# A message stage on one core: TensorE's first two layers one group further ahead, two ScalarE copies moved, sums stored an iteration later

## The reference, cut to what matters

```python
x = silu(edge_radial @ W1 + b1)          # layer 1: 8 -> 64
x = silu(x @ W2 + b2)                    # layer 2: 64 -> 64
tpw = x @ W3 + b3                        # layer 3: 64 -> 256
hs_e, hv_e = hs[src], hv[src]            # a gather: 32 features per edge
m0 = ALPHA * (einsum('eu,euw->ew', hs_e * sh0, W00) + INV_SQRT3 * einsum('eui,ei,euw->ew', hv_e, sh1, W110))
m1 = ALPHA * (einsum('eu,ei,euw->ewi', hs_e, sh1, W01) + einsum('eui,euw->ewi', hv_e * sh0, W10))
agg = segment_sum(concat(m0, m1), dst)   # then a residual and a layernorm
```

## Time and profile before

| | |
|---|---|
| median of 3 runs | 8405.06 us (8396.81 to 8455.76) |
| the profiled execution | 8418.97 us, its span 8417.1 us |
| busy over the span | PE 80%, DVE 76%, POOL 63%, ACT 33% |
| message stage | to about 4720 us |
| granted clock of TensorE, mean | 0.889 of full |

### The profile page before, as it was taken

One profiled execution on the slowest core, in us unless ns is written; L12 is line 12 of the kernel. 1 busy time (PEld: TensorE's weight loads), 2 busy tenths in 40 slices (PEclk: granted clock), 3 DMA queues, 4 the chain that ended last, 5 costly groups with the idle time before them and its releaser, 6 DMA issues.

```text
span 8417.1 us, 93644 instructions
## 1 busy us (share of the span) xinstructions
PE 6711.4 (80%) x26126; PEld 5190.8 (62%) x26126; DVE 6418.5 (76%) x11130; ACT 2817.8 (33%) x4982; POOL 5329.9 (63%) x5400
## 2 busy tenths in 40 slices
PE   6777777777777777777777409999999999999991
PEld 4555555555555555555555308888888888888881
DVE  7878887888888888887878437777777777777773
ACT  4455555555555555544444101111111111111110
POOL 5666666666666666665656566666666666666665
PEclk8888888888888888888888659999999999999995
DMA  2111111111111111111111102222222222222221
GB/s 62 41 38 42 42 42 41 41 41 40 42 42 42 42 42 41 41 38 33 35 34 35 45 24 45 48 48 50 51 48 48 51 51 48 48 49 52 48 48 27
DMA packets 318657, 363.23 MB, mean 43 GB/s; under 512 B 157446, under 2 KB 259510, under 8 KB 317962
## 3 DMA queue, kind: packets, MB, share of 16 engines
q0 software_dynamic: 175840, 136.07, 11.2%
q1 hardware_dynamic: 142794, 226.94, 8.5%
HBM read 251.38 MB, written 111.20 MB: 43 GB/s over the span
## 4 chain that ended last, share of the span: by engine, by line
PE 58%; issue 15%; another core or an unknown queue 11%; DVE 7%; ACT 6%; POOL 1%; DMA 0%; ACTq 0%; DVEq 0%; SPq 0%; POOLq 0%
PE tpw L664 29%; PE tpw L596 12%; PE hid L605 5%; PE hid L586 4%; PE hid L664 4%; PE hid L582 4%; ACT early L687 2%; ACT nearx L709 1%; ACT hid L681 1%; POOL starts L480 1%; DVE prod L964 1%; DVE hot L1255 1%; DVE early L976 1%; DVE msgs L1025 1%
## 5 line engine op out<-in xcount | busy, mean ns | idle before, releaser
L476 POOL DMA_INDIRECT early<-in_x_wide,idx x2870 | 2799.0, 975 | 1780.7 <-issue 1711.8
L476 POOL DMA_INDIRECT prod<-table,idx x2125 | 2140.7, 1007 | 1070.6 <-issue 590.2
L664 PE MATMUL tpw<-highs,hot 128*128 128x462 f32 x6125 | 2322.9, 379 | 81.1 <-DVE prod L1270 37.1
L664 PE MATMUL tpw<-lows,hot 128*128 128x462 f32 x6125 | 2302.4, 376 | 25.9 <-issue 25.2
L596 PE MATMUL tpw<-w3s,early 128*128 128x256 f32 x6252 | 1837.6, 454 | 9.4 <-DVE prod L964 9.0
L596 PEld LDWEIGHTS tpw<-w3s,early 128*128 128x128 f32 x6252 | 1379.9, 228 | 579.5 <-issue 339.0
L664 PEld LDWEIGHTS tpw<-highs,hot 128*128 128x128 f32 x6125 | 1173.0, 192 | 255.5 <-issue 58.3
L664 PEld LDWEIGHTS tpw<-lows,hot 128*128 128x128 f32 x6125 | 1167.3, 191 | 176.5 <-issue 46.4
L1270 DVE TENSOR_TENSOR prod<-tpw,mask 128x462 f32<-128x462 f32 x875 | 547.2, 637 | 540.4 <-remote 241.8
L687 ACT ACTIVATE early<-hid,b2s 64x384 f32<-64x384 f32 x1042 | 600.9, 577 | 932.8 <-PE hid L586 560.8
L582 PE MATMUL hid<-early,w1s 16*128 16x384 f32 x1044 | 552.7, 613 | 450.1 <-ACT early L687 368.8
(11 more groups left out here) (186 smaller groups left out, 7955.0 us busy)
## 6 DMA issues: line engine op xcount, KB each, us to landing
big<-qrows SPq DMA_DIRECT2D x126, 512.0 KB
scan<-prod SPq DMA_DIRECT2D x125, 425.0 KB
scan<-sums SPq DMA_DIRECT2D x130, 384.0 KB
early<-in_x_wide,idx POOLq DMA_INDIRECT x2870
prod<-table,idx POOLq DMA_INDIRECT x2125
qbx<-qx SPq DMA_DIRECT2D x131, 128.0 KB
early<-in_radial_t SPq DMA_DIRECT2D x262, 48.0 KB
sh<-in_sh SPq DMA_DIRECT2D x131, 48.0 KB
```

Source lines behind the costliest of these rows:

```text
L476: return pool.indirect_dma_start(out=dest, out_offset=None, in_=source, in_offset=bass.IndirectOffsetOnAxis(ap=index, axis=0))
L664: mm = pe.matmul(found[i % BANKS][:, 0:BC], hot(c)[:, g, at:at + P], split(s, g), start=g == 0 and s == 0, stop=g == NBATCH - 1 and s == S ...
```

## The change

PE runs layers 1 and 2 one group further ahead (`layer2(g + 2)`, `next_layer1(g + 3)`), ACT's two silus follow (`hidden(g + 2)`, `first_hidden(g + 3)`). ACT does `collect` and `spread_hv` of h1 in k1, and `spread_hv` of the next iteration's h0 in k3. POOL's wait on layer 1 names one group more. SP stores an iteration's sums after the refill two iterations later instead of one.

```diff
+            refill(1, 1, 1)
+            with sp.Fori(1, ITERS // 2 - 1) as pair:
                 for m in range(2):
-                    refill(pair * 2 + m + 1, 1 - m, 1 - m)
-                    store_sums(pair * 2 + m, m)
+                    refill(pair * 2 + m, m, m)
+                    store_sums(pair * 2 + m - 2, m)
...
                 if k % HALF == 0:
                     pool.wait_ge(tpw_ready, it * SLOTS + k - 1)
                 else:
-                    pool.wait_ge(layers_done, it * SLOTS + k)
+                    pool.wait_ge(layers_done, it * SLOTS + k + 1)
...
                     layer3(g, k % 2)
-                    layer2(g + 1)
+                    layer2(g + 2)
                     if finding and k % HALF == HALF - 1:
                         find_tile(it, m, k // HALF)
-                    next_layer1(g + 2, it + 1 if k + 2 >= SLOTS else it, (k + 2) % SLOTS)
+                    next_layer1(g + 3, it + 1 if k + 3 >= SLOTS else it, (k + 3) % SLOTS)
...
-                    hidden(g + 1, (k + 1) % 2)
-                    if k % HALF == 0:
-                        spread_hv(it, h, it > 1 if isinstance(it, int) else True)
-                    if k == 0 and before is not None:
-                        collect(it - 2, m, before, CT)
+                    hidden(g + 2, k % 2)
                     if k == 1:
+                        if before is not None:
+                            collect(it - 2, m, before, CT)
                         if first:
                             act.wait_ge(keep_ready, 1)
                         spread_keep(it, m, CT)
+                    if k % HALF == HALF - 1:
+                        spread_hv(it + 1 if h else it, 1 - h, h == 0 and before is not None or h == 1 and not first and not last,
+                                  last and h == 1)
                     if searching:
...
-                    first_hidden(g + 2)
+                    first_hidden(g + 3)
```

More of the change, by code:

```diff
@@ L406, in _ @@
                   .then_inc(qx_in[k], 16)
-            with sp.Fori(0, ITERS // 2 - 1) as pair:
+            refill(1, 1, 1)
+            with sp.Fori(1, ITERS // 2 - 1) as pair:
                 for m in range(2):
-                    refill(pair * 2 + m + 1, 1 - m, 1 - m)
-                    store_sums(pair * 2 + m, m)
+                    refill(pair * 2 + m, m, m)
+                    store_sums(pair * 2 + m - 2, m)
+            refill(ITERS - 2, 0, 0)
+            store_sums(ITERS - 4, 0)
             refill(ITERS - 1, 1)
+            store_sums(ITERS - 3, 1)
             sp.wait_ge(row_counted, SEARCHES)
@@ L622, in _ @@
             next_layer1(1, 0, 1)
+            layer2(1)
+            next_layer1(2, 0, 2)
             pe.wait_ge(w3_scaled, 1)
@@ L754, in collect, with iteration @@
                    .then_inc(sums_ready, 1)
-            def iteration(it, m, before, searching, loads=None):
+            def iteration(it, m, before, searching, loads=None, last=False):
                 first = before is None and m == 0
@@ L783, in _ @@
             first_hidden(1)
+            hidden(1, 1)
+            first_hidden(2)
+            spread_hv(0, 0, False)
             iteration(0, 0, None, True)
@@ L797, in _ @@
             iteration(ITERS - 2, 0, ITERS // 2 - 2, False, ITERS // 2 - 1)
-            iteration(ITERS - 1, 1, ITERS // 2 - 2, False)
-            spread_hv(ITERS, 0, False, True)
+            iteration(ITERS - 1, 1, ITERS // 2 - 2, False, None, True)
             collect(ITERS - 2, 0, ITERS // 2 - 1, CT)
```

## The result

| | us | iteration with the search | behind it | granted clock, whole run |
|---|---|---|---|---|
| before, median of 11 runs | 8405.7 | 35.9 | 36.0 | 0.889 |
| changed, median of 11 runs | 8482.4 | 36.8 | 35.9 | 0.856 |
| forecast | 8542 | 37.5 | 35.3 | |

The ratio is 1.0087, its 95% interval 1.0073 to 1.0102: slower by 77 us, which is real and just inside the 1% (84 us) that the prediction took as its bound. The profiled execution took 8500.6 us with a span of 8498.8, 81.7 more than before's span. The iterations account for it. With the starts of all of collect's rows it is 98 x (36.79 - 35.93) = +84 and 28 x (35.92 - 36.02) = -3, together +81.

What follows compares the result with a forecast made beforehand. A loop through VectorE, find_tile, layer 1, silus and spread_hv bounds it now; a loop between copies of h1 would follow. 98 x (37.5 - 35.9) = +157, 28 x (35.3 - 36.0) = -20: +137 on 8419, less 14: 8542 us, range 8200 to 8650.

Steps and rivals of the forecast that it cites:

- The new loop: From ScalarE's copy of h1 through silus, TensorE's layers and GpSimd's gathers to the next copy: 37.5 us with the search.
- The late signal: Layer 3 of k0' to GpSimd's first gather of h1: 5.64 us, part of it a signal late behind find_tile.
- the late signal goes: Rival at layer 3's signal to GpSimd: 2.4 us leave the loop; 8240 us, or some 7960 without clock cost; together 0.20.
- a first gather of h1 within 4 us of layer 3's start: On GpSimd behind layer 3 of k0': one of three signs that would show the prediction wrong; it took 5.64 us.
- The clock: TensorE runs at its lower level behind a 7 to 9 us pause, adding 2.5 us in layers 1 and 3.
- find_tile's stretch: On TensorE, from layer 2 of k1' through find_tile to layer 1 of k2': 0.91 + 2.98 us.
- The rival that combined them: Layer 3's signal no longer late, clock cost kept: iteration 35.1 and 32.9 us, 8240 us; 0.20 with the no-clock-cost case.
- Behind the search: Iterations after the node search: 34.05 us plus half the clock's cost, 1.25, gives 35.3; the pause a microsecond shorter.
- Collect: On ScalarE, moved to k1 before the copy of h1, where the engine would wait anyway: 2.11 us, costing nothing.
- SP's order: Stores moved back by one on SP's queue: nothing gained; unmoved, layer 1's input would come late.
- The gathers of h0: On GpSimd, landing 16 us behind the copy of h1: cost VectorE 1 to 2 us, but not the loop.
- "Remote" gone: Sign of being right, on ScalarE: the first silu no longer waits for TensorE's late layer 1 signal, 4.7 us before.

## Why the prediction was right, and where it was off

**The mechanism.** The new loop from one copy of h1 to the next sets the iteration: its terms add up in the trace (table above), it does not shorten without k1's gathers and does without k3's, and the copies taken out of it win 2.1%. The step "that closes a new loop" stands.

**The late signal, the step that was mis-sized first.** The prediction took 5.64 us from layer 3 of k0' to the first gather, "since the same instructions stand in the same order in front of it". It measured 3.62. The reason given was wrong: lateness does not come from find_tile ahead, but from the end of a run of gathers. In the kernel before layer 3's row ends at 2271.1, just as the last gather of h0' does (2271.21), and GpSimd goes on at 2273.88. In the changed kernel it ends at 2283.49 and the last gather at 2279.10. Nothing is left to hold it, and its semaphore rises at 2283.50. This is the rival "the late signal goes". It came true for this term and took 2.0 of its 2.4 us from the loop, and the prediction's own sign of being wrong, "a first gather of h1 within 4 us of layer 3's start", occurred.

**The clock, the step that was mis-sized second, the other way.** Forecast 2.5 us, measured 3.74, with the pause before it shorter (4.39 us here, 5.5 in the median) than the 7 to 9 forecast. The granted clock is 0.50 over 10.2 us, the lower level of 1.2 GHz throughout, not 0.55 over 6.6; it fell 1.1 us before the pause ended. So all but the last 0.5 us of layer 3 of k3 ran slowly, and layer 2, which the prediction's 2.5 left out. The section that the prediction named in the Trainium skill ("TensorE: Matmul & The Clock Gate", "HAM oscillation — how this bites in real kernels") has the burst behind the wait slow from its first matmul on, and here the trace agrees; its 2.8 with layer 2's 0.74 would have been 3.54.

The two errors, -2.0 and +1.2, with -0.3 on find_tile's stretch leave 36.4 for 37.5, and the forecast of +137 us became +77. That the forecast had the right sign is in part luck: with the signal's term alone put right the same sum has 35.5 and 33.3, 98 x -0.4 and 28 x -2.7, so some 115 us faster, and only the clock's error took that back. The rival that combined them (signal gone, clock paid) had 35.1; it missed by the clock's 1.2 us as well.

**Behind the search** 35.3 was forecast and 35.9 came. In 24 turns between 3800 and 4650 us the copy to the silu takes 2.33 us, 0.95 less as computed, and the gathers 12.86; layers 2 and 1 run as slowly as before, and the pause is 6.0 us in the median, not shorter. So halving the clock's cost was the error, 2 us or more, and the late signal that went hid most of it.

**Terms taken at nothing.** Collect: confirmed, since ScalarE still idles 3.31 and 5.94 us between spread_keep, which stands behind collect, and the copy of h1 in the turn above. SP's order: "if the queue were not moved, layer 1's input would come late" is true, at 890 us. The gathers of h0, "not the loop": true at 36.8, but they form a second loop at 34.1, which the prediction did not price. It bounded the kernel without k3's gathers and the one with layer 3 of k2 twice.

**The expected signs.** The copy of h1 waits for gathers in each of the 68 turns: yes, but 4.4 us in the median and not 5 or more (the 584.1 us hold the waits of h0's copy too). VectorE's waits at bsum, 300.7 us and another 182.6 in 47 waits that the profile puts down to issue, 6 us per iteration: yes. "Remote" gone: yes. Pauses of 7 us or more before one layer 2 per iteration: no, 5.5 in the median, and 7 or more in 10 of 68.

**What stays open.** Why a run of eleven gathers holds most of TensorE's signals near its end, which of them it lets pass, and by what means. The Trainium skill, "Perfetto Trace Analysis", section "Summary: the profiler window per engine type", says that a matmul's end in the profile is an estimate and that a software DMA's row ends with its descriptors, before the data has moved. By the first a late matmul would be possible too; the pairs of signals 0.13 us apart speak against it here. The second fits a release 2 us behind a gather's row, about when the copy finds the rows landed (2.41 us behind the last gather's start), and no run here separates the landing from the release. Nor were the moves of the two copies and of collect tried one at a time, and no run changed the clock alone.

## What to carry to other kernels

When a dependence is relaxed, write down the loop that closes next with every term from a row, and ask of each wait in it what else was going on at that moment: a late signal belonged here to another engine's gathers, not to the instruction ahead of it. A wait that looks idle may be pacing: letting GpSimd off its waits cost the changed kernel 5% and the one before 14%, and a store's place in a DMA queue cost 10%. Ask also which loop is second: the gain from the first ends there. TensorE's granted clock fell here from 0.87 to 0.77 when a quarter of its matmuls was cut, and the time stayed: price pauses and bursts, not matmuls.

## What the runs showed of the hardware

- In the kernel before, signals of TensorE that fall in the last 3 us of a run of gathers, or up to 1 us behind it, were late in 269 of 282 cases; the median release is 2.0 us behind the last gather's row. In the changed kernel it was 157 of 230. Where runs merge they were up to 12 us late. ScalarE's and VectorE's were in time.
- Two signals held together came 0.13 us apart in 94 of 94 pairs, though the second matmul group takes 2.86 us: the signals were held, the matmuls were done.
- The granted clock fell from 0.87 to 0.77 when 24 of the 92 matmuls of an iteration were left out, and the time stayed the same (ratio 1.0016).
- In a pause of 4.39 us TensorE's granted clock fell to its lower level, 1.1 us before the pause ended, and stayed there for 10.2 us; 12 matmuls took 5.14 us instead of 2.86.
- Five gathers fewer made the changed kernel slower by 1.3%, and the same five fewer made the kernel before faster by 2.4%.
